# A 12-stage decoder on one core: loads inside the first stage, channel queries at the scores, a fourth weight slot, output biases on POOL

## The reference

```python
x = x + _L0_attn_ref(_layernorm(x, axis=-1), ...)
x = x + _L0_xattn_ref(_layernorm(x, axis=-1), ctx_1024, ctx_1024, ...)
x = x + _L0_ffn_ref(_layernorm(x, axis=-1), ...)
...
# _L0_attn_ref, 16 heads of 8 channels
scores = jnp.einsum('bhqd,bhkd->bhqk', Q, K) / math.sqrt(HEAD_DIM)
scores = scores + _relative_bias(rel_bias, Tdim)[None]
attn = jax.nn.softmax(scores, axis=-1)
...
return out @ Wo.T + bo
# _L0_xattn_ref, 4 heads of 32 channels, c = channel
scores = jnp.einsum('bhdn,bhen->bhde', qh, kh) * scale
attn = jax.nn.softmax(scores, axis=-1)
out = jnp.einsum('bhde,bhen->bhdn', attn, vh)
...
att_global = _channel_attention(q * wqg + bqg, k * wkg + bkg, v * wvg + bvg, scale)
att_local = _channel_attention(q * wql + bql, k * wkl + bkl, v * wvl + bvl, scale)
return 2.0 * (att_global + att_local) * wp + bp
# _L0_ffn_ref: 8 experts, the two best of each token, hidden width 512
h = jax.nn.gelu(x_flat @ W1e + b1e, approximate=False)
y = h @ W2e + b2e
return (acc + ce[:, None] * y, None)
```

## Time and profile before

| | |
|---|---|
| median of 3 runs | 1593.72 us (1589.13 to 1600.24) |
| the profiled execution | 1605.27 us |
| its span in the trace | 1603.5 us, 35972 instructions |
| mean granted clock of PE | 0.803 |
| busy: PE, DVE, ACT, POOL | 1182.5, 998.0, 626.5, 617.5 us |

### The profile page before, as it was taken

The page is one execution under the profiler, slowest core; times in us unless marked ns, Lnnn a source line. Parts: engine busy times, 40 slices in busy tenths (PEclk is TensorE's granted clock), DMA queues, the critical chain, the costliest instruction groups (busy, mean ns, idle before and its releaser), DMA issues. The chain is left out here.

```text
span 1603.5 us, 35972 instructions
## 1 busy us (share of the span) xinstructions
PE 1182.5 (74%) x14256; PEld 900.2 (56%) x14256; DVE 998.0 (62%) x2808; ACT 626.5 (39%) x1479; POOL 617.5 (39%) x694
## 2 busy tenths in 40 slices
PE   6993427965999958838577882349976987667988
PEld 5663426864888845637355671348863652454656
DVE  4877731118899947861566679614439965855762
ACT  2542112422777746502365431102213534543643
POOL 3446373442233325553322314633334435415430
PEclk9975558997999979959587855569987976767989
DMA  8900024634000019003000000225530000000000
GB/s 277 160 2 1 3 93 134 188 127 128 3 3 3 3 31 180 8 19 111 27 1 1 21 9 1 84 72 181 178 113 23 2 1 1 1 2 1 2 2 27
DMA packets 72010, 89.20 MB, mean 56 GB/s; under 512 B 5823, under 2 KB 59138, under 8 KB 71200
## 3 DMA queue, kind: packets, MB, share of 16 engines
q1 hardware_dynamic: 65824, 76.95, 18.5%
q0 software_dynamic: 6016, 9.93, 1.8%
HBM read 56.62 MB, written 32.69 MB: 56 GB/s over the span
## 5 line engine op out<-in xcount | busy, mean ns | idle before, releaser
L781 POOL TENSOR_TENSOR arena<-arena,small 128x1024 f32<-128x1024 f32 x80 | 155.7, 1950 | 109.5 <-ACT arena L663 65.0
L386 POOL TENSOR_SCALAR var_eps<-moments 128x1 f32<-128x1 f32 (+1 forms) x136 | 35.7, 262 | 343.6 <-DVE moments L379 343.5
L712 ACT ACTIVATE arena<-arena 128x1024 f32<-128x1024 f32 x80 | 84.7, 1059 | 89.2 <-DVE arena L852 89.2
L737 ACT COPY arena<-ps 128x512 f32<-128x512 f32 x160 | 87.0, 589 | 67.3 <-PE ps L588 66.9
L588 PEld LDWEIGHTS ps<-small,arena 128*128 128x128 f32 x640 | 78.2, 153 | 59.7 <-ACT arena L712 34.5
L1616 PEld LDWEIGHTS ps<-expert_ring,arena 128*128 128x128 f32 (+1 forms) x864 | 104.6, 192 | 2.9
L1616 PE MATMUL ps<-expert_ring,arena 128*128 128x128 f32 (+1 forms) x864 | 104.8, 275 | 0.0
L578 PE MATMUL ps<-arena,q 64*64 64x512 f32 x640 | 92.1, 650 | 14.4 <-POOL arena L781 11.4
L588 PE MATMUL ps<-small,arena 128*128 128x128 f32 x640 | 96.0, 298 | 8.6 <-ACT arena L712 8.4
L850 DVE TENSOR_REDUCE row_max<-ps 128x16 f32<-128x1024 f32 x48 | 58.7, 1223 | 61.9 <-PE ps L578 61.6
L600 PEld LDWEIGHTS ps<-vx,arena 128*64 128x64 f32 x2560 | 87.9, 147 | 15.4 <-issue 12.8
(11 more groups left out here) (366 smaller groups left out, 2947.8 us busy)
## 6 DMA issues: line engine op xcount, KB each, us to landing
expert_ring<-L2f_in SPq DMA_DIRECT2D x23, 704.0 KB, 4.3
expert_ring<-L0f_in SPq DMA_DIRECT2D x23, 578.0 KB, 3.9
slots_L0f<-blank SPq DMA_DIRECT2D x1, 8385.0 KB, 48.7
slots_L2f<-blank SPq DMA_DIRECT2D x1, 8385.0 KB, 49.2
small<-small_in SPq DMA_DIRECT2D x1, 4167.5 KB, 19.2
expert_ring<-L1f_in SPq DMA_DIRECT2D x8, 512.0 KB, 4.0
...
```

What stands on the lines that cost most here:

```text
L712: act.activation(buf(k), buf(k), ACT.Exp, scale=exp_scale).then_inc(s.probs_ready, 1)
L737: act.copy(probsT(t)[:, j * 512:(j + 1) * 512], c.ps[:, 2 + j])\
L781: g.tensor_tensor(kx(t).rearrange("p (b h k) -> p b h k", b=2, k=S), bcast(of_tile, 2, HEADS // 2), bcast(bcast(c.w("head_of_row"), 2, S), ...
```

## The change

1. `prepare` no longer has a block of its own: it is a stage "first" in L0a's block. x comes in four loads with the weights that L0a needs (FIRST) behind the first of them, then the rest. The distance bias is loaded as a finished table `rel_bias`, `ctxT` is loaded instead of transposed.
2. The products of small weights and the tables that later layers need (`make_tables`) move into L0f, before its blocks.
3. In L0x the queries are no longer made. PE multiplies h itself with the keys of both sets (32 products of width 64 a quarter) and multiplies the query biases with the keys (64 products of width 32); ACT copies the second result (`take_bias`), and DVE joins the two with the weight as a scalar on each partition, two instructions a quarter. DVE makes the first keys of the second set, POOL the other seven sets, and adds bp after all of them. PE makes scores(q+2) ahead of values(q).
4. L0f and L1f have four weight slots, L2f three.
5. With `out_bias`, POOL adds bo to a quarter of x (`base`), and DVE's addition waits for it; the product with the row of ones goes.

```diff
-SLOTS = 3
+SLOTS = {"L0f": 4, "L1f": 4, "L2f": 3}
...
+    distance = np.arange(S)[None, :] - np.arange(P)[:, None] % S
+    bias = i["L0_attn_rel_bias"][np.clip(distance, -15, 15) + 15]
+    small["rel_bias"] = bias.transpose(0, 2, 1).reshape(P, HEADS * S)
+    small["rel_decay"] = i["L3_attn_rel_emb"][np.abs(np.clip(distance, -16, 16))]
 
-        small["L0x_wq" + s], small["L0x_bq" + s] = row(i[a + "wq" + s]), row(i[a + "bq" + s])
+        small["L0x_wq" + s], small["L0x_bq" + s] = column(i[a + "wq" + s]), row(i[a + "bq" + s])
...
+    big["ctxT"] = i["ctx_1024"].reshape(GROUP, D).T
     return small, big
...
+FIRST = ("ident", "ones", "head_of_row", "L0a_wq", "L0a_bq", "L0a_wk", "L0a_bk", "L0a_wv", "L0a_bv", "L0a_wo", "L0a_bo")
+SECOND = ("rel_bias",)
...
+
...
-            if out_bias:
-                pe.matmul(y_ps(t), c.w("ones")[0:1], c.w(n + "_bo")[0:1], start=True, stop=False)
-            pe.matmul(y_ps(t), c.oT[:, tok(t)], c.w(n + "_wo"), start=not out_bias, stop=True)\
+            pe.matmul(y_ps(t), c.oT[:, tok(t)], c.w(n + "_wo"), start=True, stop=True)\
                 .then_inc(s.y_ps, 1)
 
...
+        def base(q):
+
+            own = slice(HT * q, HT * q + HT)
+            wait_tiles(g, h_ready, HT * (q + 1))
+            g.tensor_tensor(c.x[:, own], c.x[:, own], bcast(c.w(n + "_bo"), 1, HT), ALU.add).then_inc(s.based, 1)
+
+            if out_bias and k % HT == 1 and k < nt:
+                base(k // HT)
...
-                v.tensor_tensor(buf(t), scores_ps, c.bias0[:], ALU.add).then_inc(s.scored, 1)
...
+            if out_bias:
+                v.wait_ge(s.based, t // HT + 1)
             v.tensor_tensor(x[:, t], x[:, t], y_ps(t), ALU.add).then_inc(s.y_added, 1)
...
         def scores(q):
...
+            pe.wait_ge(s.k_ready, 2 * q + 1)
+            if q == 0:
+                pe.wait_ge(s.k_first, 1)
             if q >= 2:
-                pe.wait_ge(s.shifted, q - 1)
+                pe.wait_ge(s.combined, 2 * (q - 1))
+                pe.wait_ge(s.bias_taken, q - 1)
+            keys = c.room(2 + q % 2).rearrange("p (i t d) -> p t i d", i=2, t=HT)
             for t in range(HT):
-                for i in range(2):
+                for b in range(2):
+                    for h in range(4):
+                        ch = slice(32 * h, 32 * h + 32)
+                        products = c.ps[ch, 2 * (q % 2) + b, 0:256].rearrange("p (i t e) -> p t i e", i=2, t=HT)
+                        pe.matmul(products[:, t], c.h[part(b), HT * q + t, ch], keys[part(b), t, :, ch],
+                                  start=True, stop=True, tile_position=(64 * b, 32 * h))
+            for t in range(HT):
+                for i, n in enumerate(SETS):
                     for b in range(2):
                         for h in range(4):
                             ch = slice(32 * h, 32 * h + 32)
-                            last = pe.matmul(c.ps[ch, 2 * (q % 2) + b, (2 * t + i) * 32:(2 * t + i + 1) * 32],
-                                             q_of(q, i)[part(b), t, ch], k_of(q, i)[part(b), t, ch],
+                            at = 256 + (HT * i + t) * 32
+                            last = pe.matmul(c.ps[ch, 2 * (q % 2) + b, at:at + 32],
+                                             c.w("L0x_bq" + n)[part(b), ch], k_of(q, i)[part(b), t, ch],
                                              start=True, stop=True, tile_position=(64 * b, 32 * h))
             last.then_inc(s.scores_ps, 1)
...
+        def take_bias(q):
+            act.wait_ge(s.scores_ps, q + 1)
+            if q >= 2:
+                act.wait_ge(s.combined, 2 * (q - 1))
+            act.copy(bias_part(q), bias_ps(q)).then_inc(s.bias_taken, 1)
+
...
         for q in range(QUARTERS):
             act.wait_ge(s.shifted, q + 1)
...
         for q in range(QUARTERS):
             for i, n in enumerate(SETS):
+                if q == 0 and i == 1:
+                    continue
                 if q >= 2:
                     g.wait_ge(s.scores_ps, q - 1)
+                done = 2 * q + i - (q > 0)
                 g.tensor_tensor(k_of(q, i), c.ctx_tok[:, own(q)], bcast(c.w("L0x_wk" + n), 1, HT), ALU.mult)\
                     .then_inc(s.k_scaled, 1)
-                g.wait_ge(s.k_scaled, 2 * q + i + 1)
+                g.wait_ge(s.k_scaled, done + 1)
                 g.tensor_tensor(k_of(q, i), k_of(q, i), bcast(c.w("L0x_bk" + n), 1, HT), ALU.add)\
                     .then_inc(s.k_ready, 1)
+        for q in range(QUARTERS):
             g.tensor_tensor(c.x[:, own(q)], c.x[:, own(q)], bcast(c.w("L0x_bp"), 1, HT), ALU.add)\
                 .then_inc(s.based, 1)
...
-        def queries(q):
-            if q >= 2:
-                v.wait_ge(s.scores_ps, q - 1)
-            for i, n in enumerate(SETS):
-                v.tensor_tensor(q_of(q, i), c.h[:, own(q)], bcast(c.w("L0x_wq" + n), 1, HT), ALU.mult)\
-                    .then_inc(s.q_scaled, 1)
-            for i, n in enumerate(SETS):
-                v.wait_ge(s.q_scaled, 2 * q + i + 1)
-                v.tensor_tensor(q_of(q, i), q_of(q, i), bcast(c.w("L0x_bq" + n), 1, HT), ALU.add)\
-                    .then_inc(s.q_ready, 1)
+        def first_keys():
+            v.tensor_tensor(k_of(0, 1), c.ctx_tok[:, own(0)], bcast(c.w("L0x_wkl"), 1, HT), ALU.mult)\
+                .then_inc(s.k_scaled_first, 1)
+            v.wait_ge(s.k_scaled_first, 1)
+            v.tensor_tensor(k_of(0, 1), k_of(0, 1), bcast(c.w("L0x_bkl"), 1, HT), ALU.add).then_inc(s.k_first, 1)
 
         def less_max(q):
             v.wait_ge(s.scores_ps, q + 1)
-            v.tensor_reduce(blocked(stat(q, 0)), score_ps(q), AX.X, ALU.max).then_inc(s.max_ready, 1)
-            v.wait_ge(s.max_ready, q + 1)
+            v.wait_ge(s.bias_taken, q + 1)
             if q >= 2:
                 v.wait_ge(s.turned, q - 1)
-            v.tensor_tensor(blocks_of(score(q)), score_ps(q), bcast(blocked(stat(q, 0)), 3, 32), ALU.subtract)\
-                .then_inc(s.shifted, 1)
+            for i, n in enumerate(SETS):
+                of_set = slice(i * P, (i + 1) * P)
+                v.scalar_tensor_tensor(out=score(q).rearrange("p (b n) -> p b n", b=2)[:, :, of_set],
+                                       in0=product_ps(q)[:, :, of_set], scalar=c.w("L0x_wq" + n),
+                                       in1=bias_part(q)[:, :, of_set], op0=ALU.mult, op1=ALU.add)\
+                    .then_inc(s.combined, 1)
+            v.wait_ge(s.combined, 2 * (q + 1))
+            v.tensor_reduce(blocked(stat(q, 0)), blocks_of(score(q)), AX.X, ALU.max).then_inc(s.max_ready, 1)
+            v.wait_ge(s.max_ready, q + 1)
+            v.tensor_tensor(blocks_of(score(q)), blocks_of(score(q)), bcast(blocked(stat(q, 0)), 3, 32),
+                            ALU.subtract).then_inc(s.shifted, 1)
...
-        queries(0)
-        queries(1)
+        first_keys()
+        less_max(0)
         for q in range(QUARTERS + 2):
-            if q < QUARTERS:
-                less_max(q)
-            if q + 2 < QUARTERS:
-                queries(q + 2)
+            if q + 1 < QUARTERS:
+                less_max(q + 1)
             if q < QUARTERS:
                 weights(q)
...
-            if j >= SLOTS:
-
-                sp.wait_ge(s.y_ready if n == "L0f" else s.down_ps, j - SLOTS + 1)
+            if j >= slots:
+
+                sp.wait_ge(s.y_ready if n == "L0f" else s.down_ps, j - slots + 1)
             if not capped:
                 at = sp.value_load(c.block_expert[0:1, j:j + 1], min_val=0, max_val=(E - 1) * P)
-                sp.dma_start(ring(j)[:, 0:c.row_of[n]], c.dram[n][bass.DynSlice(at, P)])\
-                    .then_inc(c.slots[n][j % SLOTS], 16)
-            elif j >= SLOTS:
+                sp.dma_start(ring(j), c.dram[n][bass.DynSlice(at, P)])\
+                    .then_inc(c.slots[n][j % slots], 16)
...
+        if n == "L0f":
+            pe.wait_ge(s.slot_of, 1)
+            for i, (a, b) in enumerate((("dq", "uq"), ("dkv", "uk"), ("kr", "qr"), ("dkv", "uv"))):
+                last = pe.matmul(c.ps[:, 0, i * P:(i + 1) * P], c.w("L2a_" + a), c.w("L2a_" + b),
+                                 start=True, stop=True)
+            last.then_inc(s.tables_ps, 1)
...
+        def make_tables():
+
+            v.tensor_tensor(c.decay3[:], c.w("rel_decay"), c.w("allowed"), ALU.mult).then_inc(s.allowed, 1)
+            v.tensor_copy(c.positions[:], c.w("pos_onehot")).then_inc(s.tables, 1)
+            v.tensor_copy(c.mask[:], c.w("causal")).then_inc(s.tables, 1)
+            v.tensor_tensor(c.gate_of_ctx[:], c.w("L2x_g1"), c.w("L2x_g2"), ALU.add).then_inc(s.tables, 1)
+            v.wait_ge(s.allowed, 1)
+            v.tensor_tensor(c.decay3[:], c.decay3[:], c.w("not_allowed"), ALU.add).then_inc(s.tables, 1)
+            v.wait_ge(s.tables_ps, 1)
+            for i in range(3):
+                v.tensor_tensor(c.q_of_h[:, i * D:(i + 1) * D], c.ps[:, 0, i * P:(i + 1) * P],
```

(53 more changed lines are left out.)

161 lines of the change are left out of this document (46 added, 115 removed).

## The result

The changed kernel takes 1555.71 us (median of 4 runs, 1552.5 to 1565.37) where the kernel before takes 1595.46 on the same chip: a ratio of 0.976, with a 95% interval of 0.972 to 0.979. It is faster by about 40 us; 42 were forecast. The profiled execution took 1556.08 us.

A forecast was written before the change was run, and what follows sets the result against it. Different engines bound each stage: PE's tables at the front, PE in L0a, DVE in L0x, PE with ring waits in L0f. 17 + 10.5 + 14.5 + 0.5 - 1 = 41.5 us, carried to the 1593.72 median: 1552 us, range 1535 to 1570.

The forecast's parts named there:

- the front: Ahead of L0a: first `shift` moves from 35.52 to about 18.4 us, 17 us gained (12 to 20).
- the slots: L0f: a fourth weight slot brings blocks from 4.50 to 3.73 us, 14.5 us gained; L1f 0.5.
- L0x: Stage L0x: DVE's work falls to 33.1 us, the stage to 44.0; 10.5 us gained (6 to 14).
- The output biases: L0a and L3a: products leaving PE gain 4 us, POOL's additions cost DVE 5; net cost 1.
- The opening: Start of L0x: DVE waits 3.4 us for the first scores (2.8) and ACT's copy (0.6).
- the 4.0 that it had ahead of the third: L0x: DVE waits another 4.0 us for quarter 2's scores, which need POOL's fifth key set at 14.7.
- the seventh set's scores: L0x: POOL's seventh key set comes at 20.6 us, its scores at 24.0, when DVE is just done.
- POOL's additions: L0a and L3a, rival: eight additions cost DVE 13.8 us instead of 5; chance 0.10, shared with L0x gaining 2.
- Transfers as the pace: L0f, rival: transfers, not slots, set the pace, so four slots give nothing; 14.5 us lost, 1567; chance 0.06.
- late loads: Front, rival: the first loads land late; 9 of the 17 us lost, 1561; chance 0.08.
- the first rival's other half: L0x, rival: POOL's keys and DVE's joining hold each other, gaining 2 us instead of 10.5; chance 0.10, shared.
- The slower side: L0a and L3a, rival: PE's clock stays low through both, together 100 us more, 1652; chance 0.02.

The follow-up runs named there:

- the kernel with no bias: The kernel after with neither output-bias products on PE nor additions on POOL in L0a and L3a: 2143.22 us, 1.344 of before (L3x ran an exact sort).
- the first stage apart: The kernel after with the first stage in its own block, so all engines meet before L0a; tables stay moved: 1581.43 us, 0.990 of before.
- The wide products: The kernel after with L0x's query-bias products made 16 a quarter of width 128 instead of 64 of width 32: 1552.43 us, 0.973 of before.
- four comparisons: Bias products put back into after (1551.65 us), with old L0x (1562.80), with wide bias products (1552.25); biases moved to POOL in the kernel before (1594.63).

## Why the prediction was right

The two largest terms, the front and the slots, were right in mechanism and size. L0x was right in kind and counted 4 us too large. The output biases came near by luck. By what was measured, 17 us of the front, 15.3 of the slots and 6.6 of L0x make 39 of the 40 us. The two profiled executions differ by 49; the one before lay 10 us above its kernel's median, and the prediction rightly carried the gain over to the median.

**The front** was counted at 17 us; the first `shift` moved by 17.05. Its steps come in the order that was forecast: POOL free at 13.26 (13.6 was read), a `scale` held on DVE for 5.33 us (4.30 was read), the `shift` behind it at 18.47 (18.4). That it comes to the tenth is luck: an earlier start and a longer hold offset each other. The longer hold is the first addition of bo, as the kernel with no bias shows (4.36, below). The prediction put the whole gain down to PE's tables. They did end last in the kernel before, but the first stage apart shows that without them the meeting would have waited for the loads almost as long. The sum had no price for that meeting, and needed none only because the change drops both.

**Four slots** were counted at 14.5 us of at most 15.4. L0f from its first row on PE to L1a's is 159.5 to 162.4 us in ten profiles with four slots and 175.6 to 176.7 in four with three: 15.3 between the means. Landing grew by 0.2 us, where 2.1 were to be had. The moved tables cost nothing that shows: L0f's part ahead of the blocks is 54.79 us before (192.55 to 247.34) and 54.81 after (159.19 to 214.00).

**L0x** is the term that was mis-sized: 10.5 counted, 6.6 measured (5.8 between the profiles of before and after). Half of the miss is DVE's own work, 35.4 us for the 33.1 of the sum. The joins write their result into SBUF, so the subtraction behind them now reads SBUF, where it read the accumulators before; beside POOL's work it took 1.66 and 1.50 us in the first two quarters, for the 0.69 of the last, and 4.9 in all for 2.8. Before and after:

```profile
L1429 DVE TENSOR_TENSOR arena<-ps,tiny 128x512 f32<-128x512 f32 x4 | 2.8, 692 | 0.1
L1467 DVE TENSOR_TENSOR arena<-arena,tiny 128x512 f32<-128x512 f32 x4 | 4.9, 1232 | 0.1
```

The other half is waiting, 13.2 us for 10.9. The opening took 4.42 us for 3.4. Ahead of the second quarter's join DVE waited 3.36 us, for which the sum had nothing; the 4.0 that it had ahead of the third didn't come, since POOL's keys are faster than counted (1.26 + 1.29 us a set for 2.94). And the step in which the seventh set's scores "come at 24.0, when DVE is just done" failed: the scores of the last quarter stand behind the first values on PE, and with stalls between small products they took 5.6 us, not 2.8, so that DVE waited 1.49 us there. The wide products confirm PE's part, 3 us of the stage.

**The output biases** came out at nothing within 1 us on the mean of four comparisons that spread from 5 us faster to 4 slower, where a net cost of 1 was counted. That this is near is luck, since neither half was right. The products are worth 3 to 6.5 us in L0a and 1.5 to 2.4 in L3a in the stages themselves, for 4 together, and the additions about 1 instead of 5. What the stages win doesn't show in the whole; the sum had no place for that.

**Port sharing.** By the rule of the Trainium skill's page "SBUF — State Buffer", section "Who interferes with whom", DVE and POOL share a port pair as an exclusive lock, which the one that issues first keeps for its whole instruction, so that an addition on POOL can hold DVE for its whole length. Had all eight done so, they would have been worth 13.8 us, the upper end of the sum. The traces agree with the lock, and show that in L0a POOL came first once in four times. That was at the front: `scale` takes 4.36 us in the kernel with no bias and 5.33 in after, where the first addition stands beside it too. The other three came when DVE's subtraction (L860) had begun, and POOL was the one held, 2.27 us for 1.28. So over L0a the subtraction takes the same with the additions as without, and over L3a 21.3 us for 20.9. The kernel with no bias at the front; after in L0a; then the subtraction over L0a in after and (as L858) with no bias:

```profile
13.56 4.36 DVE L396 TENSOR_SCALAR h<-x,moments,rstd 128x128 f32<-128x128 f32 x4 [0.47 <-POOL rstd L389]
...
60.11 1.26 DVE L860 TENSOR_TENSOR arena<-arena,row_max 128x1024 f32<-128x1024 f32 x1
60.24 2.27 POOL L789 TENSOR_TENSOR x<-x,small 128x512 f32<-128x512 f32 x1
...
L860 DVE TENSOR_TENSOR arena<-arena,row_max 128x1024 f32<-128x1024 f32 x16 | 20.2, 1261 | 0.5
L858 DVE TENSOR_TENSOR arena<-arena,row_max 128x1024 f32<-128x1024 f32 x16 | 20.2, 1261 | 0.5
```

**The rivals.** Transfers as the pace, late loads and POOL's additions are refuted by the runs above; of the first rival's other half, L0x gaining 2 us, the stage's 6.6 lies between it and the forecast. The slower side, PE at the low clock through both attention stages, didn't come: the granted clock of L0a is 0.93 after, up from 0.82, although PE has less to do there, and of L3a 0.84 as before.
